# A graph-attention kernel: the exponentials of an edge chunk in a PSUM bank, and each early spill issued a quarter into the next chunk

## The reference

```python
src = jnp.concatenate([edge_index[0], loops]); dst = jnp.concatenate([edge_index[1], loops])
e = jax.nn.leaky_relu(a_src[src] + a_dst[dst], negative_slope=0.2)
e_max = jax.ops.segment_max(e, dst, num_segments=M)
ee = jnp.exp(e - e_max[dst])
denom = jax.ops.segment_sum(ee, dst, num_segments=M)
alpha = ee / (denom[dst] + 1e-16)
agg = jax.ops.segment_sum(h[src] * alpha[:, :, None], dst, num_segments=M)
...
for ei in range(NUM_EXPERTS):
    g = jnp.where(topk_i == ei, w, 0.0).sum(-1)
    hh = jax.nn.gelu(x @ W1[ei] + b1[ei], approximate=False)
    out = out + g[..., None] * (hh @ W2[ei] + b2[ei])
```

## Time and profile before

| | us |
|---|---|
| median of 3 runs (lowest, highest) | 5322.14 (5320.33, 5331.1) |
| the profiled execution | 5313.64 |
| its span from first to last instruction | 5311.9 |
| POOL busy | 2893.2 |
| PE / DVE / ACT busy | 2631.8 / 2408.9 / 1245.7 |

### The profile page before, as it was taken

One profiled execution on the slowest core, in us unless ns is written; L12 is line 12 of the kernel. 1 busy time (PEld: TensorE's weight loads), 2 busy tenths in 40 slices (PEclk: granted clock), 3 DMA queues, 4 the chain that ended last, 5 costly groups with the idle time before them and its releaser, 6 DMA issues.

```text
span 5311.9 us, 73647 instructions
## 1 busy us (share of the span) xinstructions
PE 2631.8 (50%) x28112; PEld 1943.7 (37%) x29104; DVE 2408.9 (45%) x5226; ACT 1245.7 (23%) x2738; POOL 2893.2 (54%) x2870
## 2 busy tenths in 40 slices
PE   5667764773884677785778840023333333331000
PEld 4556653322664566564327740022222222221000
DVE  7866556677774233334457630032323232322244
ACT  2232323331442233333444420010101010100000
POOL 0000000003563677777777777777777777776773
PEclk8788877785986788897789965555555555555555
DMA  2022323570001911111431110122222222111113
GB/s 73 10 37 37 47 32 42 89 103 27 21 22 27 26 27 22 31 22 26 88 73 19 27 37 2 38 49 52 49 52 51 51 53 48 48 41 43 41 41 84
DMA packets 345120, 226.72 MB, mean 43 GB/s; under 512 B 214943, under 2 KB 302848, under 8 KB 342336
## 3 DMA queue, kind: packets, MB, share of 16 engines
q1 hardware_dynamic: 247472, 164.51, 15.8%
q0 software_dynamic: 92464, 49.28, 6.8%
q10 hardware_dynamic: 4896, 8.92, 0.7%
HBM read 136.08 MB, written 86.40 MB: 42 GB/s over the span
## 4 chain that ended last, share of the span: by engine, by line
POOL 51%; issue 19%; DVE 14%; PE 9%; DMA 4%; ACT 1%; SPq 0%; POOLq 0%; DVEq 0%; ACTq 0%
POOL arena L480 22%; POOL arena L463 18%; PE bank L494 9%; POOL arena L490 5%; POOL edge_dst_terms L472 5%; POOL arena L450 2%; DVE arena L1070 2%; DVE arena L1069 2%; DMA arena<-sort_exchange 1%; DMA early_rows<-arena 1%; DVE arena L1075 1%; DVE arena L1074 1%; DMA sort_exchange<-arena 0%; DVE arena L1207 0%; DVE arena L1179 0%
## 5 line engine op out<-in xcount | busy, mean ns | idle before, releaser
L494 PE MATMUL bank<-arena 64*64 64x64 f32 (+11 forms) x25478 | 2326.7, 295 | 1810.5 <-ACT arena L970 1203.1
L494 PEld LDWEIGHTS bank<-arena 64*64 64x64 f32 (+5 forms) x25478 | 1571.2, 165 | 1928.1 <-issue 1584.2
L480 POOL DMA_INDIRECT arena<-node_table,arena x1088 | 1158.2, 1065 | 331.6 <-issue 331.6
L463 POOL DMA_INDIRECT arena<-node_table,arena x960 | 939.5, 979 | 350.0 <-issue 288.3
L450 POOL DMA_INDIRECT arena<-sorted_keys,key_block_idx x256 | 253.5, 990 | 518.8 <-DVE key_block_idx L1212 395.1
L443 POOL IOTA arena<- 128x1024 int32 x1 | 1.0, 989 | 867.9 <-DVE h_res L1157 867.9
L494 PE MATMUL bank<-ident,arena 128*128 128x128 f32 (+2 forms) x2048 | 293.1, 316 | 255.9 <-ACT arena L950 94.4
L1412 DVE COPY arena<-arena 128x4 f32<-128x4 f32 x32 | 5.9, 183 | 808.0 <-DMA arena<-node_table,arena 807.5
L494 PEld LDWEIGHTS bank<-ident,arena 128*128 128x128 f32 (+2 forms) x2048 | 262.9, 189 | 290.5 <-DVE arena L1358 104.8
L972 ACT ACTIVATE arena<-arena 128x512 f32<-128x512 f32 x32 | 20.1, 629 | 1410.8 <-DVE arena L1420 1410.8
L490 POOL DMA_INDIRECT arena<-sums_sorted,arena x256 | 262.1, 1024 | 79.1 <-issue 77.7
(11 more groups left out here) (384 smaller groups left out, 2949.7 us busy)
## 6 DMA issues: line engine op xcount, KB each, us to landing
arena<-expert_gates SPq DMA_DIRECT2D x64, 512.0 KB, 7.6
arena<-node_table,arena POOLq DMA_INDIRECT x2048
sums_sorted<-arena SPq DMA_DIRECT2D x32, 768.0 KB, 3.3
expert_out<-arena SPq DMA_DIRECT2D x64, 256.0 KB, 2.5
arena<-expert_out SPq DMA_DIRECT2D x16, 1024.0 KB, 5.5
sort_exchange<-arena SPq DMA_DIRECT2D x14, 1024.0 KB, 3.9
early_rows<-arena POOLq DMA_DIRECT2D x15, 768.0 KB, 3.6
arena<-early_rows SPq DMA_DIRECT2D x15, 768.0 KB, 4.3
```

The lines of the kernel that those rows point to most:

```text
L463: G.indirect_dma_start(out=early_b[j%2][:,c,:],out_offset=None,in_=tbl, in_offset=bass.IndirectOffsetOnAxis(ap=gidx[:,j*CW+c:j*CW+c+1],axi ...
L480: G.indirect_dma_start(out=rch[:,j%NB,c,:],out_offset=None,in_=tbl, in_offset=bass.IndirectOffsetOnAxis(ap=gidx[:,CA+j*CW+c:CA+j*CW+c+1],a ...
L494: mm=lambda o,a,b,st=True,sp_=True: nc.tensor.matmul(o,a,b,start=st,stop=sp_,skip_group_check=True)
```

## The change

`xe` moves from SBUF to PSUM bank 5, which the second feed-forward lane gives up: that lane now has bank 4 for every expert's hidden layer, so PE waits in that lane for the gelu of expert e-1 before it computes hidden layer e. And `spill(j-1)` is issued in the middle of chunk j, after its gather number c=16 (the 17th), and no longer after the last.

```diff
-        ee=strm([CW,4]); mm_=strm([CW+1,4]); xe=strm([2*CW,4]).rearrange("p (k c) f -> p k c f",k=2); carry=strm([4,ROW])
+        ee=strm([CW,4]); mm_=strm([CW+1,4]); carry=strm([4,ROW])
...
-        YL=lanes("ffn1",2,4,first=1); take=bump(E0+NT*ROW,W2)
+        xe=PS[5][:,:].rearrange("p (k c f) -> p k c f",k=2,f=4)
+        YL=lanes("ffn1",2,4,first=1); YL[1].ps=[PS[4],PS[4],PS[6],PS[7]]; take=bump(E0+NT*ROW,W2)
...
                 for c in range(CW):
                     G.indirect_dma_start(out=early_b[j%2][:,c,:],out_offset=None,in_=tbl,
                         in_offset=bass.IndirectOffsetOnAxis(ap=gidx[:,j*CW+c:j*CW+c+1],axis=0)).then_inc(s_ga[j%2],16)
-                if j: spill(j-1)
+                    if j and c==CW//4: spill(j-1)
             spill(NCA-1)
...
                         if k=="h":
                             if e==0: pe.wait_ge(s_xld[l],16*i+16)
+                            elif l: need(pe,B,Y_STEPS,i,f"act:g{e-1}")
                             h(e,B).then_inc(B.pe,1)
```

## The result

The changed kernel takes 5147.98 us, the median of 4 runs (5143.46 to 5152.94), against 5321.24 (5316.91 to 5331.1, 4 runs) before. The ratio is 0.9677 with a 95% interval of 0.9662 to 0.9692: 3.2% faster, 173 us. The profiled execution has a span of 5141.7 us, 170.2 less than before.

A forecast was written before the change was run, and what follows sets the result against it. POOL was taken as the bound, through its issue spacing and waits. Stalls -125, spills -57 and PSUM cost +2 sum to -180, so 5322 becomes 5142, said as 5140; own range 5120 to 5165, wider 5108 to 5202.

The forecast's parts named there:

- Term 1: POOL's late gathers, held until DVE's product and scans with two SBUF inputs end, run free: 125 us gained.
- 31 x 4.2: Late edge steps: 31 steps losing 4.2 us each were to make 130 us, the whole excess of 129.8.
- Term 2: POOL's 13 waits for spills at chunk boundaries go when spills are issued 47 gathers ahead: 57 us gained.
- What is late next: POOL's second-half scatters wait for DVE's projection; POOL comes at 3159 with 9 us of slack, so the spills' gain goes through.
- Terms 3 and 4: Slower bank operands on DVE and ACT lose 2 us; the lane's rounds, 3 to 8 us longer, cost nothing on the path.
- term 3: Bank operands slow DVE and ACT, hidden for 31 steps but exposed in the last: 2 us lost.
- (a): Scans still hold POOL through their starting value and running state; only the product's stall goes: 5242 us, chance 9%.
- (b): Late stalls come from something that stays, such as the copy just ahead or writes into the chunk: 5267 us, chance 4%.
- (c): Spills' gain is eaten by the projection's wait or by spills amid gathers holding POOL as long: 5199 us, chance 4%.
- (d): Scans from a bank are so slow that DVE becomes the bound: 5814 us at 2 us more per scan, chance 2%.

The follow-up runs named there:

- e1: The changed kernel with the spills back where they were before, so only the exponentials move to the bank: 5193.49 us, ratio 0.9762.
- e4: The changed kernel with the scans' exponentials back in SBUF, the product's still in the bank: 5233.98 us, ratio 0.9842.
- e10: The changed kernel plus five kinds of DVE work in turn in late steps, the fourth 20 strided scans with one bank operand; only profile rows read.
- e6: The changed kernel plus 20 dense scans of 64 floats, both operands in SBUF, in each of 16 late steps; late gathers 1363.3 us, run not timed.
- e11: The changed kernel plus five kinds of all-SBUF scans and tensor_tensor, strided or dense, one kind a late step in turn; only profile rows read.
- e5: The changed kernel with the product's exponentials back in SBUF, the scans' still in the bank: 5159.22 us, ratio 0.9694.
- e2: The kernel before with only the spills moved a quarter into the next chunk, the exponentials still in SBUF: 5272.59 us, ratio 0.9903.
- f1: The changed kernel with the last stage's gate weights in a PSUM bank too: 5136.22 us, ratio 0.9652.
- e3: The kernel before with only the second lane's hidden layers in one bank and PE's added waits: 5319.36 us, ratio 0.9996.
- e8: The changed kernel plus five SBUF-to-SBUF copies of 1024 floats in each of 16 late steps; late gathers 8.7 us more, run not timed.
- e9: The changed kernel without 16 of the 128 scatters for the first node half: 5135.04 us, ratio 0.9645.

## Why the prediction was right

**5140 was forecast, 5148 measured**; -180 in the sum against -173 by the medians and -170.2 by the profiled spans.

*Term 1, the late stalls: 125 expected, 126.2 by the rows, 125 by e1.* A held gather is released when the product or the run of scans ends, and one bank operand removes the hold: e4 brings it back for the scans, the fourth kind of e10 shows it absent under the same strided form. Reading the end points 0.82 us apart, rather than the overlap, is what told the holding instructions from the harmless ones. The step was sound for these scans, but its wording was too broad twice. Not any two SBUF inputs do it: e6 and e11 show dense scans that hold nothing, or next to it. And not every gather that starts under a holding run is held: the prediction's own 0.98 us gather starts and ends under the scans.

The Trainium skill (SBUF — State Buffer, Who interferes with whom) says that one SBUF input does not contend outside the two-port modes: the runs with one bank operand agree (gathers of 0.94 under e10's fourth kind). Its inference that tensor_tensor leaves descriptor generation alone does not hold here: under 20 of them of 64 floats a gather took 2.79 us. Its broader statement, that two SBUF inputs contend when GpSimd reads, is wider than what dense scans showed.

Of the split inside the term the product's share, 0.82 a step, was read from one early step. In the whole trace of before the gathers that it holds lose 20.9 us, 0.81 in 23 steps and 0.29 in 8; those that the scans hold lose 103.5, and short instructions the 5.6 that remain. That 31 x 4.2 gave the whole excess is in part luck: it counts the product too high and the short instructions as nothing. Alone the product costs 0.34 a step (e5) and the scans 2.9 (e4), together less than in the kernel before, because each hold also moves the gathers that follow. What puts the gathers where the product meets them was not tried.

*Term 2, the spills: 57 expected, 51 by the rows.* From the first early gather to the first scatter it is 1299.6 us before and 1249.0 after; e1 has 1298.6, e2 1249.9; in the eleven traces with the early spill it lies between 1244.3 and 1249.9, so the term is 49 to 55 us. The mis-sized part is what had been hidden in the waits: the early gathers' busy time rises from 939.5 to 944.6, which I put down to gathers that POOL now issues where it used to stand and that fall under DVE's norms and adds. The traces bear this out: longer gathers that end 0.78 to 0.86 us behind the end of a DVE instruction lose 29.3 us in all before and 34.7 in the changed kernel. Another 1.2 us goes at the first scatter, which starts 1.75 us after the end of the last spill's issue where it was 0.55; POOL's timeline of the changed kernel:

```profile
2994.67 0.58 POOL L460 DMA_DIRECT2D early_rows<-arena  x1 [1.72 <-DMA arena<-node_table,arena]
2997.00 1.01 POOL L473 DMA_INDIRECT edge_dst_terms<-arena  x1 [1.75 <-issue]
```

*What is late next: 9 us of room expected, 10 found*, but that was luck in part. POOL comes to the wait at 3172.1, 13 us later than the forecast 3159, and the projection ends at 3162.5, 12 us later than the 3150.2 that was said not to move. From the first early gather to the projection's end it was 1408 us in the trace of before, and between 1405 and 1425 in the 13 others; it moves by itself, and the room with it. (POOL's list puts two waits of 0.3 us for that instruction in the changed kernel at the 121st and the 122nd scatter, and the chain on its page runs more through PE, 26% for 9%. I take it that the sequencer reaches the wait while earlier scatters are still being worked on; that was not tried. The room is read between the projection's end and the first scatter behind the wait.) In f1 it was 1425, and POOL stood 2.4 us for it, from its timeline:

```profile
3183.30 0.98 POOL L473 DMA_INDIRECT edge_dst_terms<-arena  x1 [2.42 <-DVE arena L1382]
```

*Terms 3 and 4: a loss of 2 us and nothing expected.* The last step, from its first instruction to SP's store, takes 11.6 us where it took 11.75, so term 3 is no loss. The lane costs nothing on the path (e3); hidden it costs 2.5 us a round, under the 3 to 8 that were expected. The price of 0.065 us for a bank operand, taken from two different operations, does not hold for scans: 20 take 5.57 us from the bank and 5.83 from SBUF.

*The sum by the rows.* Term 1 gave 126.2 and term 2 50.6, but the first early gather starts at 1742.1 us in the trace of before and at 1748.0 in that of the changed kernel, and the scatters take 0.9 more; that leaves the 170 of the spans. The 3 us between 170 and 173 are less than the spread of what lies ahead: that gather starts between 1739 and 1765 us in the 14 profiles with the same code up to it.

*The rivals.* (a), that scans hold POOL for their start or running state, is refuted by the changed kernel and by the fourth kind of e10; its price of 5242 was near, for e4, where the scans do hold POOL, took 5234. (b), copies or writes, is refuted for this size by e4 and e8, though copies do hold a little. (c): the projection's wait came in f1, with 2 us (and in e9, which leaves work out to bring it), and a spill amid the gathers costs 0.59 and 0.30, as the result shows. (d) is refuted by the scans' 5.57 us.

## What to carry to other kernels

Where POOL issues gathers one after another, look for gathers longer than the rest and compare their ends with the ends of DVE's instructions: a constant distance names the instruction that held them, and one operand in PSUM can free it. Before counting on time freed on the bound engine, find the next wait of that engine on another and how much it moves between executions. Stalls hidden behind a wait can come back when the wait goes, so take a wait's length as the upper end of what removing it gives.

## What the runs showed of the hardware that was not expected

Runs of 20 DVE scans over 64 floats with both operands in SBUF hold one of POOL's gathers when the accumulated row is strided (20 floats: gathers of 3.1 to 4.4 us) and do not when it is dense (at most 1.04), whatever the multiplier's stride, while 20 dense tensor_tensor of the same size do hold one (2.0 to 2.8 us). Both scans take about 0.2 us each. Why the row's stride decides, and why the first gather or two that start under a holding run pass, stays open.

POOL's line of 256 scatters has a gap of 2.95 to 3.5 us before the 114th and 2.97 before the 227th in all 14 traces, as in the earlier trace rows. It keeps its place in e9, which leaves out 16 earlier scatters, so it goes by their number; what it is was not tried.
